# Cross attention: heads and inverses routed through DRAM with fewer DMAs, and two steps moved between queues

## The reference, cut to what matters

```
q = Wq @ x + bq;  k = Wk @ ctx + bk;  v = Wv @ ctx + bv        # 16 heads of 16 channels, 512 positions
dot = mask * (q . k) / 4 - (1 - mask) * 1e6                    # 512 x 512 a head
out = (softmax(dot) * mask) @ v                                # 256 x 512
x   = layernorm(x + out)                                       # over the 512 positions
```

## Time and profile before

| what | value |
|---|---|
| runs | 3818.95, 3791.48 and 3818.0 us, median 3818.0 |
| the profiled execution | 3803.1 us, span of its instructions 3801.3 us |
| clock granted to TensorE over the span | 0.909 |
| the cross attention changed here | about 453 to 1309 us of the span |
| busy over the span | PE 82%, DVE 44%, ACT 33%, POOL 14% |

### The profile page before, as it was taken

One profiled execution on the slowest core, in us unless ns is written; L12 is line 12 of the kernel. 1 busy time (PEld: TensorE's weight loads), 2 busy tenths in 40 slices (PEclk: granted clock), 3 DMA queues, 4 the chain that ended last, 5 costly groups with the idle time before them and its releaser, 6 DMA issues. The chain is left out here.

```text
span 3801.3 us, 48719 instructions
## 1 busy us (share of the span) xinstructions
PE 3109.5 (82%) x16306; PEld 2055.6 (54%) x16339; DVE 1682.5 (44%) x3232; ACT 1257.8 (33%) x3220; POOL 546.1 (14%) x551
## 2 busy tenths in 40 slices
PE   6999647786766469999978888599999997799894
PEld 5666422222222157777755555488888886444441
DVE  5666534554545222211215666366666665211113
ACT  2333214444444311111104444355565553111110
POOL 1000200111110120000000000233333332300002
PEclk9999867877888689999989999799999998999997
DMA  1000174434444220000010000211121113500323
GB/s 67 12 22 22 53 133 81 93 79 87 92 93 72 68 82 23 12 12 12 12 47 12 22 22 17 100 40 45 46 81 63 45 33 114 226 0 33 121 88 108
DMA packets 123827, 227.30 MB, mean 60 GB/s; under 512 B 14392, under 2 KB 27192, under 8 KB 123664
## 3 DMA queue, kind: packets, MB, share of 16 engines
q1 hardware_dynamic: 107488, 186.54, 18.3%
q0 software_dynamic: 7664, 27.40, 2.1%
q10 hardware_dynamic: 8512, 11.20, 1.0%
HBM read 157.36 MB, written 63.01 MB: 58 GB/s over the span
## 5 line engine op out<-in xcount | busy, mean ns | idle before, releaser
L1261 DVE TENSOR_REDUCE x_minus_max<-banks 128x2 f32<-128x1024 f32 x256 | 308.8, 1220 | 266.7 <-PE banks L1325 261.4
L1206 ACT ACTIVATE x_probs<-banks 128x512 f32<-128x512 f32 x512 | 285.9, 595 | 283.6 <-PE banks L1343 223.4
L1343 PE MATMUL banks<-x_stacked_q,x_stacked_k 53*128 53x512 f32 x512 | 254.7, 560 | 106.0 <-ACT x_probs L1206 70.0
L1325 PE MATMUL banks<-x_stacked_k,x_stacked_q 51*128 51x512 f32 x512 | 204.1, 529 | 106.2 <-DVE x_minus_max L1261 79.4
L1343 PEld LDWEIGHTS banks<-x_stacked_q,x_stacked_k 53*128 53x128 f32 x512 | 100.7, 220 | 350.1 <-ACT x_probs L1206 178.4
L481 ACT ACTIVATE a_probs<-banks,a_minus_max 128x128 f32<-128x128 f32 (+1 forms) x512 | 209.0, 425 | 146.7 <-DVE a_minus_max L564 144.7
L1355 PE MATMUL banks<-x_probs,x_v 128*32 128x512 f32 x1024 | 174.5, 760 | 6.6 <-ACT x_probs L1206 6.6
L2142 ACT ACTIVATE x_probs<-banks,x_minus_max,x_rroot 128x256 f32<-128x256 f32 x256 | 143.1, 566 | 91.4 <-DVE x_minus_max L2253 91.4
L2078 POOL TENSOR_TENSOR x_probs<-x_probs,x_inverse 128x512 f32<-128x512 f32 x128 | 133.3, 1041 | 275.3 <-DVE x_inverse L2287 275.3
L564 DVE TENSOR_REDUCE a_minus_max<-banks 128x2 f32<-128x512 f32 (+1 forms) x192 | 131.8, 686 | 83.8 <-remote 55.7
L2812 DVE TENSOR_TENSOR m_h<-banks,m_silu 128x512 f32<-128x512 f32 x39 | 27.0, 691 | 318.1 <-PE banks L2928 165.2
(11 more groups left out here) (369 smaller groups left out, 7684.5 us busy)
## 6 DMA issues: line engine op xcount, KB each, us to landing
x_parts_dram<-x_parts SPq DMA_DIRECT2D x16, 1024.0 KB, 5.0
x_x<-x_after SPq DMA_DIRECT2D x24, 512.0 KB, 4.5
x_stacked_k<-x_parts_dram SPq DMA_DIRECT2D x48, 256.0 KB
x_stacked_q<-x_parts_dram SPq DMA_DIRECT2D x48, 256.0 KB
x_after<-a_z SPq DMA_DIRECT2D x16, 512.0 KB, 2.8
x_z<-x_after SPq DMA_DIRECT2D x16, 512.0 KB, 7.4
x_after<-x_z SPq DMA_DIRECT2D x16, 512.0 KB, 2.8
x_context<-in_ctxT SPq DMA_DIRECT2D x16, 512.0 KB, 5.5
```

Source lines behind the costliest of these rows:

```text
L1206: act.activation(probs[:, n % 8, :], psum[at.bank(f"exp{n}")], ACT.Exp, scale=SCALE)\
L1261: dve.tensor_reduce(minus_max[:, c % 2, h % 4:h % 4 + 2, t], at.pair(use), AX.X, ALU.max, negate=True)\
L1325: ins = pe.matmul(at.pair(use)[:, half, :], stacked[0][to][rows, h, t * P:(t + 1) * P].bitcast(F32R), stacked[1][to][rows, h, :].bitcast(F ...
L1343: ins = pe.matmul(psum[at.bank(use)], stacked[1][u][rows, h // 2, s * P:(s + 1) * P].bitcast(F32R), stacked[0][u][rows, h // 2, :].bitcast ...
```

## The change

- `move_heads` (eight DMAs a group) becomes `write_heads`: one DMA of the whole group, 128 x 512, to `heads_dram`. `read_heads` brings, for a half, the sums and the channels back with one DMA each. `fold_sums` is gone.
- On SP, the read of half 1 of batch b-1 stands ahead of `stack(b+1)`; SP waits there until the group has landed in DRAM.
- `spread_inverse` leaves SP. Two new steps on ACT take its place: "send" (waits for the reciprocal, one DMA to `inverse_dram`) and "spread" (waits until that has landed, one DMA that repeats all eight rows over 128 partitions).
- The slots: `inverse''` 15 to 18, then `send''` 20, `spread''` 24; `stats''` 4 to 6 and 36 to 40, `normalise''` 42 to 46, "inverse" 48 to 50, then "send" 52, "spread" 56.
- ACT's copy of a group waits for the write of two groups earlier; POOL's `combine` waits for the read and for the one spread.

```diff
-        for step, at in ((("stats''", 0), 4), (("inverse''", 1), 15), (("stats''", 1), 36), (("normalise''", 0), 42), (("inverse", 0), 48)):
+        for step, at in ((("stats''", 0), 6), (("inverse''", 1), 18), (("send''", 1), 20), (("spread''", 1), 24), (("stats''", 1), 40),
+                         (("normalise''", 0), 46), (("inverse", 0), 50), (("send", 0), 52), (("spread", 0), 56)):
...
+            def write_heads(b, u, c):
+
+                sp.wait_ge(heads_copied, b * 4 + (c + 1))
+                sp.dma_start(heads_dram[u, c], heads_out[:, c % 2, :]).then_inc(heads_written[c % 2], 16)
+
+            def read_heads(b, u, n):
+
+
+                for k in range(2):
+                    sp.wait_ge(heads_written[k], b * 32 + (n + 1) * 16)
+                if n == 0 and not (isinstance(b, int) and b == 0):
+                    sp.wait_ge(combine_steps, b * COMBINE_STEPS - COMBINE_STEPS // 2)
+                by_head = heads_dram[u, 2 * n:2 * n + 2].rearrange("c (i q) s -> (c i) q s", q=32)
+                sp.dma_start(sums[:, n, :], by_head[:, CH, :].rearrange("h (k f) -> h k f", f=P)).then_inc(sums_loaded[n], 16)
+                sp.dma_start(heads[:, n, :], by_head[:, 0:CH, :]).then_inc(heads_read[n], 16)
...
                 if prev:
-                    move_heads(b - 1, 1 - u, 3)
+                    write_heads(b - 1, 1 - u, 3)
+                    read_heads(b - 1, 1 - u, 1)
                 if following:
                     stack(b + 1, 1 - u)
-                if prev:
-                    fold_sums(b - 1, 1 - u, 1)
...
-                if prev:
-                    spread_inverse(b - 1, 1 - u, 1)
                 if own:
-                    move_heads(b, u, 0)
-                    move_heads(b, u, 1)
-                    fold_sums(b, u, 0)
+                    write_heads(b, u, 0)
+                    write_heads(b, u, 1)
+                    read_heads(b, u, 0)
                 if prev:
                     store(b - 1, 1 - u)
                 if own:
-                    spread_inverse(b, u, 0)
-                    move_heads(b, u, 2)
+                    write_heads(b, u, 2)
...
+                    if kind in ("send", "send''"):
+                        owner, of = (b, u) if kind == "send" else (b - 1, 1 - u)
+                        act.wait_ge(inverted, owner * 2 + (n + 1))
+                        act.dma_start(inverse_dram[of, n].rearrange("h (k f) -> (h k) f", f=P), inverse[:, n, :]).then_inc(inverse_written[n], 16)
+                    if kind in ("spread", "spread''"):
+                        owner, of = (b, u) if kind == "spread" else (b - 1, 1 - u)
+                        act.wait_ge(inverse_written[n], owner * 16 + 16)
+                        act.dma_start(inverse_rows[:, n, :], inverse_dram[of, n].unsqueeze(1).broadcast_to([H // 2, CH, POS]))\
+                            .then_inc(inverse_loaded[n], 16)
```

More of the change, by code:

```diff
@@ L966, in cross_attention_masked @@
         heads_copied = sem("heads_copied")
-        heads_moved = [sem(f"heads_moved{k}") for k in range(2)]
-        sums_loaded = sem("sums_loaded")
+        heads_written = [sem(f"heads_written{k}") for k in range(2)]
+        heads_read = [sem(f"heads_read{n}") for n in range(2)]
+        sums_loaded = [sem(f"sums_loaded{n}") for n in range(2)]
         inverted = sem("inverted")
-        inverse_written = sem("inverse_written")
-        inverse_loaded = sem("inverse_loaded")
+        inverse_written = [sem(f"inverse_written{n}") for n in range(2)]
+        inverse_loaded = [sem(f"inverse_loaded{n}") for n in range(2)]
         combine_steps = sem("combine_steps")
@@ L1066, in stack @@
                             .then_inc(stacked_ready[w][u], 16)
-            def move_heads(b, u, c):
-                n, half = c // 2, c % 2
+            def write_heads(b, u, c):
                 sp.wait_ge(heads_copied, b * 4 + (c + 1))
-                for i in range(4):
-                    sp.dma_start(sums_dram[u, n, 4 * half + i:4 * half + i + 1, :], heads_out[32 * i + CH:32 * i + CH + 1, half, :])\
-                        .then_inc(heads_moved[half], 16)
-                for i in range(4):
-                    sp.dma_start(heads[64 * half + CH * i:64 * half + CH * (i + 1), n, :], heads_out[32 * i:32 * i + CH, half, :])\
-                        .then_inc(heads_moved[half], 16)
-            def fold_sums(b, u, n):
-                for half in range(2):
-                    sp.wait_ge(heads_moved[half], (b * 2 + (n + 1)) * MOVES)
-                sp.dma_start(sums[:, n, :], sums_dram[u, n].rearrange("h (k f) -> (h k) f", f=P)).then_inc(sums_loaded, 16)
-            def spread_inverse(b, u, n):
-                sp.wait_ge(inverted, b * 2 + (n + 1))
-                sp.dma_start(inverse_dram[u, n].rearrange("h (k f) -> (h k) f", f=P), inverse[:, n, :]).then_inc(inverse_written, 16)
-                sp.wait_ge(inverse_written, (b * 2 + (n + 1)) * 16)
-                for h in range(H // 2):
-                    sp.dma_start(inverse_rows[CH * h:CH * (h + 1), n, :], inverse_dram[u, n, h].unsqueeze(0).broadcast_to([CH, POS]))\
-                        .then_inc(inverse_loaded, 16)
+                sp.dma_start(heads_dram[u, c], heads_out[:, c % 2, :]).then_inc(heads_written[c % 2], 16)
[7 more added lines that the diff above has]
+                sp.dma_start(heads[:, n, :], by_head[:, 0:CH, :]).then_inc(heads_read[n], 16)
             load_inputs(0, 0)
@@ L1160, in combine @@
                 s = (b * 2 + n) * (COMBINE_STEPS // 2)
-                for half in range(2):
-                    pool.wait_ge(heads_moved[half], (b * 2 + (n + 1)) * MOVES)
-                pool.wait_ge(inverse_loaded, (b * 2 + (n + 1)) * 16 * (H // 2))
+                pool.wait_ge(heads_read[n], b * 16 + 16)
+                pool.wait_ge(inverse_loaded[n], b * 16 + 16)
                 pool.tensor_tensor(heads[:, n, :], heads[:, n, :], inverse_rows[:, n, :], ALU.mult).then_inc(combine_steps, 1)
@@ L1285, in run @@
                         owner = b if kind == "inverse" else b - 1
-                        dve.wait_ge(sums_loaded, (owner * 2 + (n + 1)) * 16)
+                        dve.wait_ge(sums_loaded[n], owner * 16 + 16)
                         dve.reciprocal(inverse[:, n, :], sums[:, n, :]).then_inc(inverted, 1)
```

5 lines of the change are left out of this document (2 added, 3 removed).

## The result

The changed kernel takes 3820.22 us (median of 20 runs, 3803.96 to 3833.08) against 3805.03 us for the kernel before (median of 20, 3791.48 to 3818.95). The ratio is 1.0033, with a 95% interval of 1.0017 to 1.0048: some 13 us (0.3%) slower, where 22 us faster had been forecast. The profiled execution has a span of 3824.0 us, 22.7 above that of before.

What follows compares the result with a forecast made beforehand. DVE's wait for sums queued behind stacked rows was taken to stall PE, then the slot-24 loads. Terms 22 + 5 + 5 - 5 - 1 - 4 = 22 us faster: 3796 against the median, own range 3770 to 3822.

Steps and rivals of the forecast that it cites:

- The bound and its successor: Batches 1 to 6: DVE's wait for sums stalls PE, 74.0 us; next PE waits at slot 24 for the context.
- (A): Rival: inputs don't hold PE at slot 24, all 74.0 us go; 69 us faster, 3749; chance 0.12.
- (C): Rival: sums still come late and DVE stands as before, only costs remain less the end; 3823; chance 0.08.
- the price of the channels' read: 256 KB read ahead of the stacked rows delays the loads 1.4 us a batch, between 0.8 and 1.9 us.
- the 25 us of room: Batches 1 to 5: loads land 4 to 6 us before PE reaches slot 24, bounding the gain to 25 us.
- The start of the stacked rows: SP's queue: stacked rows start 4.0 us behind group 3's copy, not 4.8, so 0.8 us earlier.
- the clock: PE's granted clock could move any term, up to 5 us a batch, 25 in all, either way.
- ACT's issues and waits: ACT's DMA issues cost 5 us, two more in batch 7 1 us, the wait at slot 56 4 us.
- some 8 us more that batch 6 would miss: Batch 6: ACT's wait at slot 24 leaves about 5 us kept, 13 if the send lands at once.
- Rival D: ACT's small DMA overtakes SP's queue, lands in 1.4 us; batch 6 keeps 13 us, not 5; 3788; chance 0.10.
- rival B: Spread at slot 56 waits 9 us in six batches, 54 us in place of 4; 3846; chance 0.10.
- The end: Behind the last batch: shorter chain starts POOL's last product 5 us sooner, 3 to 6.

Runs made afterwards that it cites:

- SP's spread: Changed kernel with the send and spread of the inverses given back to SP, one DMA each: 3803.06 us, ratio 0.9995.
- both costs undone: Changed kernel with the channels' read behind the loads for batch b+2, and the inverses sent and spread by SP: 3786.10 us, ratio 0.9947.
- the loads first: Changed kernel with the loads for batch b+2 issued ahead of the stacked rows: 3722.66 us, ratio 0.9777.
- place of the parts' writes: Changed kernel, but SP waits for the spread of half 0 (slot 56) before it writes the parts of batch b+2: 3825.17 us, ratio 1.0024.
- the slots: Kernel before with the new slots of the reciprocals, statistics and normalisation alone: 3794.53 us, ratio 0.9949.
- the path through memory: Kernel before with heads through memory alone: one write a group, sums and channels read back by one DMA each behind the stacked rows: 3792.03 us, ratio 0.9937.
- the sums ahead: Kernel before with one edit, the DMA of the sums of half 1 issued ahead of the stacked rows: 3796.90 us, ratio 0.9976.
- the loads first in the kernel before: Kernel before with the loads for batch b+2 ahead of the stacked rows, the sums still behind them: 3807.79 us, ratio 0.9984.

## Why the prediction was wrong, point by point

**The bound and its successor were right.** DVE's stall went whole, and PE then stood at slot 24 for the context, as forecast, 13.7 us a batch where 9 to 11 stood. The rival that the inputs wouldn't hold PE (A) is refuted by the 68.5 us; that the sums would still come late (C) by DVE's missing wait.

**The first term that failed is the price of the channels' read.** I took 1.4 us a batch and an earlier start of 0.8. Measured: the stacked rows start 3.0 us into the batch against 3.4, 0.4 sooner, and 44.5 us pass from there to slot 24 against 39.7 to the landing before (five batches each), so 4.8 us more. Net 4.4, not 0.6: the 25 us of room were spent, and the 22 of the forecast came out at about 3 (48.1 against 47.5). Not all of the 4.8 is the read: with it moved away the loads land 3.8 us sooner (47.4 to 43.6), and 4.4 us sooner with SP's spread (46.5 to 42.1). Putting the read elsewhere gave 24 us (18 us with ACT's share undone first). My upper bound of 1.9 us was for bytes at a rate of all engines. The Trainium skill's rule on the number of engines (DMA: Bandwidth & Descriptors, "Why a DMA increments its semaphore by 16 and not by 1"), which I had put into a sentence by itself, pointed the right way, and the share of 0.45 behind the last batch bears it out. Half of the engines for all of the bytes would make twice the 1.9 us, 3.8 us; that is an estimate from the two, and no run separates it from the other ways in which a read in front can delay a queue. The start of the stacked rows had a slip of its own: 0.4, 2 and 0.8 us are 3.2, and I wrote 4.0. Measured it is 3.9 us behind the copy of group 3, 4.4 before.

**The second weighs more, and is a step that I didn't see as one: that what is won ahead of slot 24 is kept to the end of the batch, with the clock put at nothing.** It isn't kept. In the changed kernel the rest of the batch takes 59.8 us, not 53.5: 31 us in five batches, against the 3 us won ahead of slot 24. With both costs undone PE starts 5.5 us sooner and ends the batch when it always did. PE is busy 51 us behind slot 24 and not 44, for the same matmuls, at a clock of 0.75 and not 0.89, while its idle time there stays at 8 to 9 us. I had named the clock, with up to 25 us either way, but left it out of the sum, as if the sign were open. What sets the level is settled in part at most. The first 8 us behind slot 24 are slow (0.57 against 0.89) where PE comes out of the stall right there; shortening the stall by 20 matmuls left it so. The last 16 us (0.64 against 0.90) are slow without that stall too (0.67 with the loads first). The place of the parts' writes isn't it (0.73). ACT's steps (0.79 without them), the slots (0.80), the path through memory (0.83), the sums ahead (0.83) and even the loads first in the kernel before (0.82) each go with a part of it, on one profile each. No run separates a cause there, and why the clock falls late in the batch stays open.

**ACT's issues and waits** were put at 5 + 1 + 4 us, with some 8 us more that batch 6 would miss. Measured 14 and 17 us: right in size, in part by luck. In batches 1 to 5, 15 of the 17 us that go with them are PE's busy time at the clock (400.9 to 385.8), a path that the forecast had not put a price on, and batch 6 shrinks by 2 us only (77.9 to 75.8); the 8 us show there once the read is out of the way too (77.8 to 70.0). ACT at slots 20 to 24 in batch 6 of the changed kernel:

```profile
1199.39 0.33 ACTq L1220 DMA_DIRECT2D x_inverse_dram<-x_inverse  x1
...
1209.62 0.65 ACTq L1224 DMA_DIRECT2D x_inverse_rows<-x_inverse_dram  x1
1210.36 1.08 ACT L1192 ACTIVATE x_probs<-banks 128x512 f32<-128x512 f32 x2 [5.93 <-DMA x_inverse_dram<-x_inverse]
```

The send lands 10.2 us behind its issue (14.4 was my nearest row), and ACT stands 5.9 us. Batch 6 shrinks from 84.5 to 77.9 us, 6.6 against 5 forecast; in the second profiles from 90.0 to 80.7. Rival D, in which ACT's small DMA overtakes SP's backlog, would have it land in 1.4 us; it took 10.2 us and in batch 1 11.1 (662.46 to 673.55). From the Trainium skill's round of the queues (DMA: Bandwidth & Descriptors, "Queues, rings and completion order") I had worked out an early landing; the trace doesn't show one. Where the 10 to 11 us go is not shown.

**Slot 56 (rival B).** In batch 1 the send is issued at 724.24 and the spread at 730.94, 6.7 us, where 5.9 was forecast and 14.4 would have been the rival. The send lands 5.2 us behind its issue, before ACT gets to slot 56, so from batch 1 on ACT waits for nothing there: the 4 us that I put on this term are nothing. B is refuted; it isn't what made the kernel slower.

**The end.** POOL's product starts 11.1 us behind the last copy of a group (1314.84 to 1325.91), where it was 14.6 (1287.43 to 1302.00): 3.5 us, in the bounds of 3 to 6, under the 5 taken.

In sum: the parts without the two costs give 20 us (0.9947) where the forecast's terms had 43 (25 + 13 + 5); the channels' read takes 18 where 3 stood; ACT takes 14 where 18 stood. 20 - 18 - 14 is 12 us slower, the measured 13; this sum closes by construction, as its terms are steps from one run to the next. The clock is in each of them: it isn't a fourth term. And the number itself shows nothing: 3820 lies in my own range of 3770 to 3822 only because three runs of before had a median of 3818.0, where twenty have 3805.03. Neither of my two signs of being wrong showed up, a PE that doesn't wait at slot 24 or an ACT that waits around slot 56: both watched waits, and the loss came as longer busy time.

## What to carry to other kernels

When a stall goes, ask where the next one ends and what stands ahead of it in the same queue: here two stalls stood behind one block of transfers, worth 9 us and nothing alone and 98 us together, and the order of three calls in SP's queue was the whole of it. Weigh each DMA that is put ahead of such a block by the time to the landing behind it, not by its bytes over the mean rate; a read with eight rows outermost moved that landing by 3.8 to 4.4 us where its bytes say 1 to 2. And don't carry a gain in the middle of a clock-bound stretch to its end at face value: compare PE's busy time for the same matmuls in both profiles, over the whole stretch. Here 39 us less waiting came back as 39 us more of it.

## What the runs showed of the hardware

- TensorE's granted clock over the second half of a batch differs by kernel and repeats: 0.89 and 0.90 in two profiles of the kernel before, 0.75 and 0.74 in two of the changed one, with the same matmuls and nearly the same idle time. It makes PE's busy time there 51.7 us and not 44.2.
- The level did not rise when 8.7 us of an idle stretch of 14 us were filled with matmuls (0.72); 5.7 us of idle time were left right ahead of slot 24.
- In the 8 us behind slot 24 the granted clock was 0.54 to 0.67 in the mean of five batches in all the profiles in which PE stood until slot 24, and 0.81 and 0.89 in the kernel before, whose stall had ended earlier.
- Over five batches the same 1520 matmuls kept PE busy for 362.4 us at a mean granted clock of 0.77 (kernel before) and for 401.4 us at 0.70 (both costs undone), while its idle time fell from 145.6 to 106.8 us.
- A 256 KB read from DRAM into 128 partitions with eight heads outermost ran at 176 GB/s and a DMA share of 0.45 with nothing beside it, a 256 KB write from 128 partitions at 386 GB/s and 1.01. Ahead of the stacked rows the read moved the landing of the loads by 3.8 to 4.4 us, and by 3.6 when it was split into eight DMAs of 16 rows, which took SP 3.7 us to issue.
- Beside SP's backlog a 16 KB DMA of ACT's queue landed 10.2 and 11.1 us behind its issue, beside the parts' writes in 5.2 us, and in 1.4 us at slot 52 of batch 7, which has neither.
- Three edits that each made the kernel 0.2 to 0.6% faster alone were worth 0.5% together, with intervals of 0.15 to 0.2% either way.
